# A pre-norm linear attention and int8 FFN block: a transposed copy of x as a further input, LayerNorm's numbers spread by a transfer, and new call orders

## What is computed

```
x = x + attn(layernorm(x), qkv_w, qkv_b, out_w, out_b)
x = x + ffn(layernorm(x), weight_int8, weight_scale, bias)

attn: q, k, v = split(x @ qkv_w.T + qkv_b)          # 16 heads of 32
      q = relu(q) + 1e-6 ; k = relu(k) + 1e-6
      kv = cumsum(einsum('bhld,bhle->bhlde', k, v)) ; k_cum = cumsum(k)
      out = (q . kv) / max(q . k_cum, 1e-6)         # causal linear attention
      return out @ out_w.T + out_b
ffn:  x_scale = max(|x|.max() / 127, 1e-5)          # one number for the whole of x
      x_int8 = clip(round(x / x_scale), -128, 127)
      return (x_int8 @ weight_int8.T) * x_scale * weight_scale.T + bias
```

## Time and profile before

| | |
|---|---|
| median of 3 runs | 1075.56 us (1075.49 to 1076.29) |
| the profiled execution | 1075.05 us, of it 1073.3 us span of the instructions |
| busy, share of the span | PE 98%, PE weight loads 73%, DVE 75%, ACT 68%, POOL 81% |
| granted PE clock, mean | 0.998 of full speed |
| DMA | 120.69 MB, 112 GB/s on the mean |

### The profile page before, as it was taken

One profiled execution on the slowest core, in us unless ns is written; L12 is line 12 of the kernel. 1 busy time (PEld: TensorE's weight loads), 2 busy tenths in 40 slices (PEclk: granted clock), 3 DMA queues, 4 the chain that ended last, 5 costly groups with the idle time before them and its releaser, 6 DMA issues.

```text
span 1073.3 us, 29299 instructions
## 1 busy us (share of the span) xinstructions
PE 1047.6 (98%) x10735; PEld 779.6 (73%) x10735; DVE 806.8 (75%) x1603; ACT 727.8 (68%) x1319; POOL 866.1 (81%) x1094
## 2 busy tenths in 40 slices
PE   5999999999999999999999999999999999998998
PEld 3777777778778777777787877877777777764554
DVE  5867777778787778777777777777777777698776
ACT  6776666676676666666766766666667667654997
POOL 2579887878788888888788887888788888893998
PEclk9999999999999999999999999999999999999999
DMA  7323343333333333333333333333333333233995
GB/s 274 80 50 93 97 109 94 86 81 91 92 90 90 86 92 97 100 88 88 91 87 87 88 92 90 87 100 99 90 87 81 90 91 93 51 117 103 383 403 211
DMA packets 74976, 120.69 MB, mean 112 GB/s; under 512 B 16465, under 2 KB 16977, under 8 KB 74834
## 3 DMA queue, kind: packets, MB, share of 16 engines
q1 hardware_dynamic: 74304, 118.29, 37.6%
q10 hardware_dynamic: 530, 0.54, 0.2%
HBM read 36.97 MB, written 31.46 MB: 64 GB/s over the span
## 4 chain that ended last, share of the span: by engine, by line
PE 93%; DVE 3%; ACT 1%; issue 1%; DMA 1%; POOL 1%; SPq 0%; DVEq 0%; ACTq 0%; POOLq 0%
PE unit L737 30%; PE unit L750 15%; PE misc L818 14%; PE acc L2188 5%; PE sc L786 5%; PE o_st L874 4%; PE o_st L840 3%; PE o_st L849 3%; PE unit L720 3%; PE misc L804 2%; PE unit L770 2%; PE o_st L854 2%; PE tp L2178 1%; PE acc L2193 1%; DMA stack<-qkv_wt 1%
## 5 line engine op out<-in xcount | busy, mean ns | idle before, releaser
L737 PE MATMUL unit<-xt_hi,w_hi 128*128 128x256 f16 x1000 | 273.0, 273 | 2.4 <-ACT relu L1159 2.2
L737 PE MATMUL unit<-xt_hi,w_lo 128*128 128x256 f16 x1000 | 272.9, 273 | 0.0
L737 PE MATMUL unit<-xt_lo,w_hi 128*128 128x256 f16 x1000 | 272.9, 273 | 0.0
L1159 ACT ACTIVATE relu<-unit,qk_bias_scaled 128x256 f32<-128x256 f32 x250 | 117.5, 471 | 152.1 <-PE unit L737 151.6
L1612 DVE SCALAR_TENSOR_TENSOR x_ring<-sc,x_ring 128x512 f16<-128x512 f32 x256 | 174.3, 684 | 46.8 <-ACT x_ring L1201 44.0
L506 POOL TENSOR_TENSOR qk_lo<-f_t,qk_hi 128x512 f16<-128x512 f32 x128 | 148.4, 1160 | 56.1 <-ACT qk_hi L1178 56.1
L1201 ACT ACTIVATE x_ring<-sc 128x512 f16<-128x512 f32 x256 | 148.0, 591 | 59.0 <-PE sc L786 59.0
L523 POOL TENSOR_SCALAR_AFFINE_SELECT x_ring<-x_ring 128x512 f16<-128x512 f16 x256 | 164.3, 642 | 26.4 <-DVE x_ring L1612 26.1
L525 POOL TENSOR_SCALAR_AFFINE_SELECT x_ring<-x_ring 128x512 f16<-128x512 f16 x256 | 168.0, 656 | 0.0
L737 PEld LDWEIGHTS unit<-xt_hi,w_hi 128*128 128x128 f16 x1000 | 97.8, 98 | 20.7 <-ACT relu L1159 3.0
L737 PEld LDWEIGHTS unit<-xt_lo,w_hi 128*128 128x128 f16 x1000 | 97.9, 98 | 16.4
(11 more groups left out here) (224 smaller groups left out, 2711.0 us busy)
## 6 DMA issues: line engine op xcount, KB each, us to landing
stack<-qk_hi SPq DMA_DIRECT2D x504, 64.0 KB, 2.0
xs<-x SPq DMA_DIRECT2D x64, 256.0 KB, 2.7
stack<-qk_lo SPq DMA_DIRECT2D x256, 64.0 KB, 2.0
out<-res SPq DMA_DIRECT2D x64, 256.0 KB, 5.3
x_spill<-xs SPq DMA_DIRECT2D x56, 256.0 KB, 2.3
x_ring<-x_spill SPq DMA_DIRECT2D x56, 256.0 KB, 5.6
stack<-qkv_wt SPq DMA_DIRECT2D x6, 512.0 KB, 8.2
x_ring<-out_wt SPq DMA_DIRECT2D x1, 1024.0 KB, 12.1
```

Source lines behind the costliest of these rows:

```text
L737: mm = pe.matmul(dst[:, 0:GT], wp[:, k, f:f + P], xp[:, g % 2, k, :], start=(n == 0), stop=(n == len(terms) - 1))
L1159: act.activation(relu[:, i % 4, :], src[:, 0:GT], ACT.Relu, bias=qk_bias_scaled[:, f:f + 1]).then_inc(qk_done, 1)
```

## The change

- **A further input.** The host supplies `x_turned`, x with tokens and features exchanged for each batch (16.8 MB). From the fifth chunk on (4 to 63) the features of a pair come on partitions by a transfer (`load_turned`, 512 KB, 1 KB runs). The rows for LayerNorm's statistics come by one more transfer for each pair (`load_rows`, 512 KB), and the row loads for the residual stay.
- **LayerNorm's numbers.** Mean and inverse deviation of a pair are stored to DRAM (`store_ln`, 512 elements of four bytes) and read back spread over all 128 partitions (`spread_ln`, 256 KB).
- **Normalising.** DVE does it in two TENSOR_TENSOR on SBUF for each chunk (`centre_x`, `scale_x`) in place of one TENSOR_SCALAR. ACT and DVE split x from SBUF, no longer from PSUM.
- **PE** transposes x for the first four chunks alone. `project_v` waits for the low part of its own chunk. The bank table has 12 users.
- **Order.** New lists for all engines. The projections run one pair further ahead of the attention, LayerNorm's statistics some seven pairs ahead, and `x1_moments` up to seven chunks behind.
- **Small things.** `own_head` is a quarter of its size and made at the start; the scaled bias of v overwrites v's bias; `wo_stage` lies in `xs`, so that the first batch's later rows load after the out weights are split; some semaphores are merged; `add_bias` waits for the load of its rows.

```diff
@@ transfers
+                def load_rows(g, since=3):
...
+                    if g >= 4:
+                        sp.wait_ge(ln_stats, upto(GROUP * (g - 2) + 1))
...
+                    sp.dma_start(xa[:, g % 2, :, :], x_pairs[g]).then_inc(xa_loaded[g % 2], 16)
+                def load_turned(g, since=3):
...
+                    if g >= 4:
+                        sp.wait_ge(xt_lo_done, upto(GROUP * (g - 2) + 1))
+                    sp.dma_start(x_tr[:, g % 2, :, :], x_turned_of[g]).then_inc(turned_loaded[g % 2], 16)
+                def store_ln(g, since=3):
...
+                    sp.wait_ge(ln_step, (g + 1) * LN_STEPS)
+                    sp.dma_start(ln_rows[g].rearrange("k c p -> p (k c)"), mrv[:, g % 2, 0:2, :].rearrange("p k c -> p (k c)"),
+                                 allow_slow_non_contiguous=True).then_inc(ln_stored[g % 2], 16)
+                def spread_ln(g, since=3):
...
+                    sp.wait_ge(ln_stored[g % 2], g // 2 * 16)
...
+                    sp.dma_start(ln_of[:, g % 2, :, :].rearrange("p k t -> p (k t)"),
+                                 ln_rows[g].rearrange("k c p -> (k c p)").partition_broadcast(P)).then_inc(turned_loaded[g % 2], 16)
@@ the loop of PE
-                for n in range(6, N - 4, GROUP):
+                for n in range(8, N - 2, GROUP):
...
-                    transpose_x(n + 3)
...
-                    transpose_x(n + 4)
@@ PE, project_v
+                    if g > 0:
+                        pe.wait_ge(xt_lo_done, upto(GROUP * g + j))
@@ PE at the start
                 sum_squares(0)
+                sum_squares(2)
                 first_unit(0)
-                sum_squares(2)
@@ DVE
+                def centre_x(c, since=AHEAD):
...
+                    dve.wait_ge(turned_loaded[g % 2], g // 2 * 32)
+                    dve.tensor_tensor(turned(c), turned(c), spread(c, 0), ALU.subtract).then_inc(x_centred, 1)
+                def scale_x(c, since=AHEAD):
...
+                    dve.wait_ge(x_centred, upto(c - AHEAD))
+                    dve.tensor_tensor(turned(c), turned(c), spread(c, 1), ALU.mult).then_inc(xt_ready, 1)
```

More of the change, by code:

```diff
@@ L927, in _ @@
                 project_v(0, 1, 0)
+                project_v(1, 0)
+                sum_out_squares()
                 project_qk(1, 0)
@@ L1106, in _ @@
[L1106 to L1111 removed]
+                project_qk(4, 0)
+                keys_values(4, 1)
+                project_qk(4, 1)
+                project_qk(4, 2)
+                transpose_keys(5)
+                outputs(4, 0)
+                scores(5, 2)
+                scores(5, 3)
+                outputs(4, 1)
@@ new lines, in _ @@
+                keys_values(5, 0)
+                project_out(3)
+                project_v(4, 1)
+                project_qk(4, 3)
+                scores(6, 0)
+                scores(6, 1)
+                outputs(5, 0)
+                outputs(5, 1)
+                transpose_attn(4)
+                scores(6, 2)
+                project_qk(4, 4)
+                keys_values(5, 1)
+                transpose_keys(6)
+                project_qk(4, 5)
+                project_out(4)
+                project_qk(4, 6)
```

1214 lines of the change are left out of this document (657 added, 557 removed).

## The result

The changed kernel takes 1113.52 us (median of 3 runs, 1108.35 to 1118.37) against 1075.56 us (1075.49 to 1076.29): a ratio of 1.035, with a 95% interval of 1.0275 to 1.0425. The forecast was 1064 us and a range of 1053 to 1080. Not only the sign is wrong: the runs now lie 10 us apart where they lay 0.8 us apart before. The profiled execution is the slowest of the three, 1118.37 us, so what follows explains 43.3 us and not the 38 between the medians.

What follows compares the result with a forecast made beforehand. PE's list of work was taken as the bound, with DVE's pace at the end of stage 1. 1075.05 - 26.4 + 3.3 + 3.5 + 7.9 = 1063.4 profiled, so 1064 us; range 1053 to 1080.

Steps and rivals of the forecast that it cites:

- What PE loses: On PE, the transposes of 60 chunks go at 0.44 us each, all on the path: 26.4 us less.
- SP and the transfers: Four more transfers a pair and LayerNorm's four-byte store fit SP's and DMA's free time: cost zero at both ends.
- The start: Among the first pairs, later units and a stack wait, less old stalls: +3.5 us, bounds 0 and 8.
- the squares: At the start, the third weight's squares go ahead of PE's first unit, so units begin about 2.3 us later.
- The steady stack wait: In the steady part, a pair's first scores sometimes wait for stack transfers: +3.3 us, bounds 0 and 15.
- the margin of 0.8 us: Spare time between stack transfers landing and a steady pair's first scores, down from 5.0 us; most pairs do not wait.
- DVE's load: Six two-input SBUF operations a pair at 1.0 us each make DVE 92% busy, still below PE: cost zero.
- the thin cover: In the steady part, DVE's 26.0 us against PE's 28.3 us a pair leave only 2.3 us.
- that rule of the Trainium skill: VectorE instructions with two SBUF inputs and GpSimd ones reading SBUF exclude each other for a whole instruction: up to 1.9 us.
- the 1.9 us of the rival: DVE becomes the bound through POOL: at 1.9 us an operation, 31.4 us a pair and 1151 us; chance 0.10.
- The end of stage 1: At the last pair, PE waits 8.4 us for stacks, then DVE sets the pace: +7.9 us, bounds 3.5 and 10.
- the stacks come late: In every pair PE waits at first scores, from ACT's late split or SP; about 1088 or 1074 us; chance 0.14.

Runs made afterwards that it cites:

- nostore: Changed kernel without the stores of LayerNorm's numbers, the spreading load reading a row of x instead (output not the reference's): 1078.15 us, ratio 1.0022.
- nostore_ends: nostore with three orders turned back: first unit before third weight's squares, ACT's third split before eighth feature, chunk 59's output projection before last pair's scores: 1076.10 us.
- ln8: Changed kernel with LayerNorm's numbers stored as 256 pieces of 8 bytes, DVE reading them at a step of two elements: 1081.37 us, ratio 1.0056.
- ln16: Changed kernel with LayerNorm's numbers stored as 128 pieces of 16 bytes, DVE reading them at a step of four elements: 1095.91 us, ratio 1.0186.

## Why the prediction was wrong, point by point

**What PE loses: right.** 240 transposes are gone and PE's work ahead of T0 is 18.8 us less; nostore reaches T0 2.3 us before the kernel before in spite of 16.5 us more lost time. The sign that I had named, PE's busy time down by 26 us, did not come: it fell by 3.8 us in the changed kernel and by 16.4 in nostore. A busy time is no measure of the work where the clock differs: a matmul of L846 takes 385 ns on the mean where its kind took 379.

**SP and the transfers: the step that failed.** I wrote that no transfer of four-byte pieces is in the trace, took the stack transfer's 2.0 us as the nearest row, said that ten times of it would still fit the loop's lead of two pairs, and set the cost to zero at both ends. The price was bounded at 20 us and the one seen in the chain, 9 to 13 us, lay inside. Wrong was what I compared it with. First, the lead of two pairs is that of the loop. At the start SP's list has the store and the load of the same pair with a few stack parts between them: SP itself waited 19.1 us in four places for the store, all in the first 200 us (its queue's waits, in the changed kernel):

```profile
SPq L389 <- DMA ln_rows<-mrv: 19.1, 4, 6.3
```

Second, I priced the store for its own reader and not for the transfers behind it, which it held on both queues (10.4 us for ACT's, where it was 2.0, and 2.9 without the stores). The runs put 32 to 35 us of the 38 on it.

**The start: 12.0 us by nostore where I had 3.5 with a bound of 8.** I had costed two waits. One, the squares, is disproved by nostore_ends; the other, 3.1 us ahead of pair 1's first scores, is not in nostore's trace, where PE does not stand still there. I had not added up that the statistics of seven pairs and the two-tensor operations of the first chunks fall into the same 100 us; that explains 3 us of the 12. The rest stays open.

**The steady stack wait: right in kind.** Without the store 4.5 us are lost from 200 us to T0, for +3.3 and bounds of 0 and 15. Between 200 us and T0 the first scores of a pair wait for 0.5 us at most in nostore, as the margin of 0.8 us said, and most do not wait; in the changed kernel, with the stores, some wait for 1.0 and one for 2.6.

**DVE's load: right.** x was taken as 1.0 us with bounds 0.69 and 1.90; the three groups above give (870 + 727 + 1050) / 3 = 882 ns. DVE is busy for 174.47 of 200 us, 87% for 92%. On the mean POOL and DVE hold each other up by tenths, as the prediction took it, and the thin cover held. Single operations show more (shortest, median and longest ns in the changed kernel):

```profile
L1732 DVE TENSOR_TENSOR xt_lo<-x_ring,xt_hi x60: 677/685/1644, 69.0 to 938.7; 128x512 f16<-128x512 f32 x60
```

Of these 60, 26 took 1276 to 1644 ns, and these are just the ones that began while a POOL operation still had more than 0.5 us to run. So a hold of nearly the rest of a POOL operation, as by that rule of the Trainium skill, does occur. It strikes 26 times in 60 here, and the mean of the three lines stays far from the 1.9 us of the rival.

**The end of stage 1: the place right, its make-up and size wrong.** T0 to the scores of chunk 62 is 13.5 us (forecast 12.5). PE stands still in it for 7.6 us, and I had 8.4, all of it for the stacks. The changed kernel's waits there name four reasons:

```profile
PE sc L882 <- DMA stack<-qk_lo: 4.2, 1, 4.2
PE sc L882 <- DVE x_ring L1755: 2.4, 1, 2.4
PE o_st L936 <- POOL x_ring L613: 0.7, 1, 0.7
PE o_st L970 <- DVE state L1875: 0.3, 1, 0.3
```

From these scores to the largest value it is 38.1 us where I had 33.8. That figure was added up wrongly: 31.5, 1.2 and 2.6 make 35.3. nostore and ln8 have 36.2 and 36.8. The chain of the changed kernel:

```profile
969.64 3.95 PE unit L830 x36
...
987.11 0.58 PE sc L882 x4
987.70 5.13 PE misc L914 x12
...
1025.18 0.34 PE acc L2374
```

The 12 matmuls of an output projection take 5.13 us at 987.70, where they take 2.59 otherwise, and the four scores ahead of them 0.58 where they took 0.23: the granted clock is 0.67 and 0.86 in the two stretches of 10 us from 980 on, after and among these waits. These two rows alone are 2.9 us that no term of mine had. The same shows at 100 to 200 us (0.91).

**The sum without the store.** 1063.4 for the profiled execution, plus 8.5 at the start, 1.2 in the steady part and 2.6 behind T0, gives 1075.7; nostore's profiled span of 1073.9 with before's 1.75 outside it is 1075.65. So with the store's price at zero, as I had it, the change would still have gained nothing.

**The chances.** The rival "the stacks come late" had the right witness (transfers) for a wrong reason, and no rival had the stores. No version run here beats the kernel before.

## What to carry to other kernels

A transfer is priced twice: for who reads it, and for every other transfer that is under way or behind it, on other queues too. A store in four-byte pieces is tried at once with a layout that makes the pieces 8 bytes, which took away 32 of some 35 us here. A lead that a loop gives is not there among the first pairs, so an operation that is new to a pipeline is costed at the start from the start's own list. A layout that helps the transfer can hurt the reader, so both are to be looked at in the same trace. And a long wait is split by what ended each part of it before its removal is priced: behind the wait for the stacks stood one for DVE.

## What the runs showed of the hardware

- A store of 256 pieces of 4 bytes to DRAM added in 34 places costs this kernel 21 us, and one of 256 pieces of 8 bytes 0.8 (interval -0.5 to +1.5 us), with equal packet counts. Added to the kernel before, stores of 2 KB land in 2.7 us (128 pieces of 16 bytes) and 4.1 us (256 of 8 bytes). In the changed kernel's places they land in 6.5 us (ln16) and 7.6 us (ln8), and with 512 pieces of 4 bytes they take 9 to 13 us in its chain.
- While such a four-byte store is out, transfers of another queue are held (10.4 us for 64 KB, against 2.9 without the stores), and the DMA engines are mostly idle (share 0.22 from 42 to 51 us, against 0.82).
- A fp32 tensor_tensor of 512 elements on DVE with two inputs in SBUF takes 870 ns on the mean beside POOL's work with the second input read without a step (shortest 681), 892 at a step of two elements (674) and 1304 at a step of four (1075).
- With waits of 0.3, 2.4, 0.7 and 4.2 us within 13.5 us, PE's granted clock is 0.67 in the stretch from 980 to 990 us, and the next 12 matmuls of 512 columns take 5.13 us instead of 2.59 (1.2 for 2.4 GHz).
